# A state-space stage with four input products turned by TensorE and six C products on GpSimd

## The reference

```
u, z   = split(layernorm(x_mod) @ W_in.T)          # 512 + 512 channels
u      = silu(causal_conv4(u))
dt_in, B, C = split(u @ W_x.T, [64, 16, 16])
dt     = clamp(softplus(dt_in @ W_dt.T + b_dt))     # 512
h[n]   = exp(-A[n] * dt) * h[n] (token before) + (dt * u) * B[n]
y      = sum over n of h[n] * C[n]  +  D * u
out    = (y * silu(z)) @ W_out.T, then residual and gate
```

## Time and profile before

| | us |
|---|---|
| median of three runs | 4106.91 |
| profiled execution, first to last instruction (the page gives no other time for it) | 4108.2 |
| DVE busy in the span | 3549.2 |
| POOL busy | 2624.4 |
| PE busy | 3305.6 |
| ACT busy | 2321.0 |

### The profile page before, as it was taken

How to read it: one execution, slowest core, us unless ns; L and a number is a source line. 1 busy time by engine, 2 the same in 40 slices (tenths; PEclk the granted TensorE clock), 3 DMA queues, 4 the chain that set the end, 5 groups by cost and what they waited for, 6 DMA issues and landing times. The chain is left out here.

```text
span 4108.2 us, 61159 instructions
## 1 busy us (share of the span) xinstructions
PE 3305.6 (80%) x21708; PEld 1529.2 (37%) x21708; DVE 3549.2 (86%) x5829; ACT 2321.0 (56%) x4302; POOL 2624.4 (64%) x2459
## 2 busy tenths in 40 slices
PE   5979999999993999999566777777777777776467
PEld 3633333333332555555322232222232232222166
DVE  5768888888854999999359999999999999999967
ACT  5626666666672344444356666666666666666422
POOL 1102323232232888888369999999999999998723
PEclk8969999999996999999888888888888888887689
DMA  4894565655513111110112222212222222222132
GB/s 146 281 188 64 78 84 79 88 80 81 82 33 89 35 44 45 44 48 30 34 44 61 63 65 64 69 47 60 69 65 64 65 69 61 68 57 53 42 95 85
DMA packets 274957, 299.58 MB, mean 73 GB/s; under 512 B 35583, under 2 KB 205686, under 8 KB 274646
## 3 DMA queue, kind: packets, MB, share of 16 engines
q1 hardware_dynamic: 274654, 295.68, 31.4%
HBM read 210.22 MB, written 84.51 MB: 72 GB/s over the span
## 5 line engine op out<-in xcount | busy, mean ns | idle before, releaser
L1727 POOL TENSOR_TENSOR d_dBu<-d_dtu,d_Bn 128x1024 f32<-128x1024 f32 x512 | 1217.5, 2413 | 0.1
L1562 ACT ACTIVATE d_dA<-d_dt,d_decay 128x512 f32<-128x512 f32 x1024 | 690.9, 687 | 404.4 <-DVE d_h L1810 402.1
L752 ACT ACTIVATE b_P<-b_pT 128x512 f32<-128x512 f32 (+1 forms) x1120 | 571.8, 575 | 298.1 <-PE b_pT L658 295.3
L1810 DVE TENSOR_TENSOR_SCAN d_h<-d_dA,d_last_h,d_dBu 128x512 f32<-128x512 f32 x512 | 617.1, 1265 | 14.5 <-ACT d_dA L1562 12.8
L1810 DVE TENSOR_TENSOR_SCAN d_h<-d_dA,d_dBu 128x512 f32<-128x512 f32 x512 | 586.3, 1204 | 40.3 <-ACT d_dA L1562 39.0
L785 DVE CUSTOM_DVE_ANT_0 b_pS<-b_pS,mask_qk 128x512 f32<-128x512 f32 (+1 forms) x768 | 501.7, 690 | 83.6 <-PE b_pS L668 74.3
L630 POOL TENSOR_SCALAR_AFFINE_SELECT b_P<-b_P 128x128 f32<-128x128 f32 (+2 forms) x608 | 192.8, 321 | 515.0 <-ACT b_P L752 503.2
L668 PE MATMUL b_pS<-KS,QS 99*128 99x512 bf16 (+3 forms) x1536 | 475.0, 339 | 28.5 <-PEq L85 21.6
L658 PE MATMUL b_pT<-QS,KS 118*128 118x512 bf16 (+3 forms) x1536 | 449.1, 329 | 3.1 <-ACT b_P L752 2.1
L1817 DVE TENSOR_TENSOR d_h<-d_h,d_C 128x2048 f32<-128x2048 f32 x192 | 434.4, 2262 | 0.7 <-PE d_C L1446 0.7
L1446 PE MATMUL d_C<-d_bc,d_pick 96*128 96x512 bf16 x256 | 114.6, 448 | 396.1 <-DVE d_h L1817 396.1
(11 more groups left out here) (313 smaller groups left out, 5983.2 us busy)
## 6 DMA issues: line engine op xcount, KB each, us to landing
d_Bn<-scratch_bs SPq DMA_DIRECT2D x128, 512.0 KB, 4.9
scratch_parts<-a_part SPq DMA_DIRECT2D x48, 512.0 KB, 4.1
QS<-scratch_parts SPq DMA_DIRECT2D x192, 128.0 KB, 7.4
KS<-scratch_parts SPq DMA_DIRECT2D x192, 128.0 KB, 7.9
scratch_v<-a_v SPq DMA_DIRECT2D x16, 1024.0 KB, 7.7
V<-scratch_v SPq DMA_DIRECT2D x32, 512.0 KB, 11.7
a_x<-in_L_attn_x_dram SPq DMA_DIRECT2D x16, 512.0 KB, 7.7
scratch_o<-b_O SPq DMA_DIRECT2D x16, 512.0 KB, 10.0
```

Of the source, the lines that this page charges most:

```text
L752: act.activation(t[:, heads[0]:heads[-1] + 1, c * CH:c * CH + w], pT[:, place % RING, 0:len(heads) * w].rearrange("p (h w) -> p h w", w=w) ...
L1562: act.activation(dA[:, m % 2, :], dt[:, c.k % 2, m, :], ACT.Exp, scale=decay[:, m, n:n + 1]).then_inc(dA_d, 1)
L1727: pool.tensor_tensor(product(c, n)[:, 2 * j:2 * j + 2, :], dtu[:, c.k % 2, 2 * j:2 * j + 2, :], Bn[:, n // BG % 2, n % BG, :].unsqueeze(1) ...
L1810: dve.tensor_tensor_scan(h[:, n % HS, m, :], dA[:, m % 2, :], product(c, n)[:, m, :], start, ALU.mult, ALU.add).then_inc(scanned, 1)
```

## The change

Four states, PE_B = (5, 8, 11, 14), get their product dtu * B[n] another way. dtu is turned once per chunk into [token, channel] layout: PE makes 16 transposes of 128x128 into the y banks (`turn_step`), ACT copies them to `dtuT` in two parts (`put_step`), and B likewise goes through pC into `BT` (`turn_b`, `put_b`). In that layout B[n] is one number per partition, so the product of a state is four instructions of [128, 512] with a scale per partition: by ACT for states 8 and 14 (`stage_product`), by POOL's `tensor_scalar` for 5 and 11. PE then turns each product back, 4 transposes for each m, into the slots of `dA` in PSUM (`turn_product`), and the decays of the two first m of such a state go to a new SBUF tile `dAs` (as do the others of that state). The scan reads decays from `dAs` and products from `dA`.

POOL_C becomes (0, 3, 6, 8, 10, 12). The C rows for POOL no longer come from pC by ACT but by DMA from scratch (`bs` now holds C too) into three slots `Cn`. `modulate` goes from DVE to POOL, joined with `shift`. x2e is gone: `finish` adds into h1, and SP loads x2 into h1 only after the front's second norm. The orders of all engines are rewritten: ACT has one turn function per m, with entries behind each; PE has three places in a turn; POOL's `weigh` is behind the entries of its turn. The masks of attention go to another allocation scope, which moves addresses.

```diff
-POOL_C = (0, 3, 6, 11)
+PE_B = (5, 8, 11, 14)
+POOL_B = tuple(n for n in range(NS) if n not in PE_B)
+POOL_C = (0, 3, 6, 8, 10, 12)
+LAG, KEEP, AHEAD = 2, 1, (7, 5, 4, 1)
+POOL_P = (5, 11)
+ACT_P = tuple(n for n in PE_B if n not in POOL_P)
@@ SP
+            def spread_c(at, j):
+                slot = at.times(NPC, j) % CR
+                row = NS + POOL_C[j]
+                wait(sp, hC_pool, at.times(NPC, j + 1 - CR))
+                sp.dma_start(Cn[:, slot, :], S["bs"][row:row + 1, tokens(at)].to_broadcast([P, CH])).then_inc(cn_in[slot], 16)
...
                     for g in range(2):
                         if c is not None:
-                            wait(sp, dBu_d, c.times(2 * NS, 2 * (NS - BG + BG * g)))
+                            wait(sp, dBu_d, c.times(2 * NPB, MADE[NS - BG + BG * g]))
                         spread_b(q, g)
+                        if g == 0:
+                            spread_c(q, CR - 1)
                 if e is not None:
+                    wait(sp, xn2, min(total, e.times(1, 4)))
+                    wait(sp, h1_st, 16 * min(total, e.times(1, 4)))
+                    sp.dma_start(h1[:, :, :], tiles(S["x2"][tokens(e), :])).then_inc(x2_in, 16)
                     wait(sp, x3_d, e.times(1, 1))
-                    sp.dma_start(tiles(S["x3"][tokens(e), :]), x2e[:, :, :]).then_inc(stored, 16)
+                    sp.dma_start(tiles(S["x3"][tokens(e), :]), h1[:, :, :]).then_inc(stored, 16)
@@ PE
+            def turn_step(c):
+                wait(pe, dtu_d, c.times(1, 1))
+                wait_before(pe, yz_d, c.times(1, 0), passed)
+                for t in range(CT):
+                    for m in range(MD):
+                        last = pe.transpose(y[:, t, m * P:(m + 1) * P], dtu[:, c.k % 2, m, t * P:(t + 1) * P], K["ident"][:, :])
+                    if t % 2:
+                        last.then_inc(dtuT_mm, 1)
+            def turn_product(c, n, halves):
+                i = PE_B.index(n)
+                if n in POOL_P:
+                    wait(pe, staged_pool, c.times(CT * len(POOL_P), CT * POOL_P.index(n) + CT))
+                else:
+                    wait(pe, staged, c.times(CT * len(ACT_P), CT * ACT_P.index(n) + CT))
+                for m in halves:
+                    wait(pe, scanned, c.times(NS * MD, MD * n + m - 1))
+                    for t in range(CT):
+                        last = pe.transpose(dA[:, m % 2, t * P:(t + 1) * P], product(c, n)[:, t, m * P:(m + 1) * P], K["ident"][:, :])
+                    last.then_inc(turned_b, 1)
@@ PE order
             run(pe, spread,
+                ({},
+                 {1: turn_b, 2: own_input},
+                 {1: lambda q: project(q, IN + 3, 3), 4: lambda q: convolve(q, 1), 9: lambda q: project_dt(q, 2), 13: lambda q: (project(q, GT + 1, MD + 1), project(q, GT + 2, MD + 2))},
+                 {15: lambda f: turn(f, 1)}),
+                sums_dve,
                 ({6: lambda e: output(e, 0)},
+                 {},
+                 {1: lambda q: convolve(q, 0), 4: lambda q: convolve(q, 2), 5: lambda q: convolve(q, 3), 7: project_x, 14: lambda q: project(q, GT + 3, MD + 3)},
+                 {14: lambda f: turn(f, 0)}),
+                sums_pool,
                 ({10: lambda e: output(e, 1)},
+                 {1: turn_step},
+                 {0: lambda q: project(q, IN + 2, 2), 8: lambda q: (project_dt(q, 0), project_dt(q, 1)), 9: lambda q: project_dt(q, 3), 11: lambda q: project(q, GT + 0, MD + 0)},
+                 {15: lambda f: (project(f, IN, 0), project(f, IN + 1, 1))}))
@@ ACT
+                for of in ACT_P:
+                    if MD * n + m in [MD * of - back for back in AHEAD]:
...
+                        act.activation(product(c, of)[:, t, :], dtuT[:, t, :], ACT.Identity, scale=BT[:, t, of:of + 1]).then_inc(staged, 1)
...
-                 {3: lambda f: normalise(f, 0, (0, 1)), 10: lambda f: normalise(f, 1, (0,)), 11: lambda f: normalise(f, 1, (2,)),
+            run(act, decays(0),
+                ({},
+                 {2: put_b},
+                 {1: lambda q: inner(q, 2), 4: lambda q: convolved(q, 1), 8: take_x, 9: lambda q: below(q, 0), 13: lambda q: gate(q, 1)},
+                 {9: lambda f: normalise(f, 1, (0,)), 14: lambda f: normalise(f, 1, (3,)), 15: lambda f: turned(f, 0)}),
+                decays(1),
                 ({0: last_gate},
+                 {},
+                 {3: lambda q: convolved(q, 0), 6: lambda q: convolved(q, 3), 7: silu, 8: split_hi, 9: lambda q: below(q, 1), 10: lambda q: (below(q, 3), grow(q)), 11: split_mid, 14: lambda q: gate(q, 2)},
+                 {5: lambda f: normalise(f, 0, (0, 1)), 13: lambda f: normalise(f, 1, (2,)), 15: lambda f: turned(f, 1)}),
...
+                 {2: lambda c: (put_step(c, 0), put_step(c, 1))},
@@ POOL
+                if n in POOL_P:
+                    wait(pool, scanned, before(c, n))
+                    wait(pool, dtuT_put, c.times(2, 2))
+                    wait(pool, bt_put, c.times(1, 1))
+                    for t in range(CT):
+                        pool.tensor_scalar(product(c, n)[:, t, :], dtuT[:, t, :], BT[:, t, n:n + 1], None, ALU.mult).then_inc(staged_pool, 1)
+                for j in range(2 if n in POOL_B else 0):
...
+            def modulate(f):
+                wait(pool, m_in[f.k // 2 % 2], f.over(4, 16, 16))
+                wait(pool, xn1, f.times(1, 1))
+                pool.tensor_tensor(x[:, :, :], x[:, :, :], row(f, CA), ALU.mult).then_inc(h_mul, 1)
...
             def finish(e):
-                wait(pool, e_in, e.times(32, 32))
+                wait(pool, x2_in, e.times(16, 16))
                 wait(pool, ag_d, e.times(2, 2))
-                pool.tensor_tensor(x2e[:, :, :], x2e[:, :, :], h1e[:, :, :], ALU.add).then_inc(x3_d, 1)
+                pool.tensor_tensor(h1[:, :, :], h1[:, :, :], h1e[:, :, :], ALU.add).then_inc(x3_d, 1)
@@ DVE
                 for m in range(MD):
-                    if m % 2 == 0:
-                        wait(dve, dBu_d, c.times(2 * NS, 2 * n + m // 2 + 1))
+                    if n in PE_B:
+                        wait(dve, turned_b, c.times(MD * NPE, MD * PE_B.index(n) + m + 1))
+                    elif m % 2 == 0:
+                        wait(dve, dBu_d, c.times(2 * NPB, MADE[n] + m // 2 + 1))
```

More of the change, by code:

```diff
@@ L1356, in step @@
                         else:
-                            for chunk, parts in zip((e, q, f), turn):
+                            for chunk, parts in zip((e, c, q, f), turn):
                                 if chunk is not None and n in parts:
@@ L1403, in step @@
[L1403 to L1412, removed]
+                for n in range(NS):
+                    if n == 0 and f is not None:
+                        load(f)
+                    if c is not None:
+                        if n % BG == 0 and 0 < n < NS - BG:
+                            spread_next(c, n // BG + 1)
+                        for j in range(CR, NPC):
+                            if POOL_C[j - CR] + 3 == n:
+                                spread_c(c, j)
+                    if n == 8 and f is not None:
+                        wait(sp, h1_d, f.times(1, 1))
+                        sp.dma_start(tiles(S["r"][tokens(f), :]), h1[:, :, :]).then_inc(h1_st, 16)
+                    if n == 10 and q is not None:
+                        wait(sp, act_read, q.times(NF, WX + 1))
+                        sp.dma_start(S["bs"][:, tokens(q)], xb[DR:DR + 2 * NS, :]).then_inc(b_st, 16)
@@ L1836, in stats @@
                 last.then_inc(stat, 1)
-            def modulate(f):
-                wait(dve, m_in[f.k // 2 % 2], f.over(4, 16, 16))
-                wait(dve, xn1, f.times(1, 1))
-                dve.tensor_tensor(x[:, :, :], x[:, :, :], row(f, CA), ALU.mult).then_inc(h_mul, 1)
             def clear(f):
@@ L1872, in gate_out @@
                 dve.tensor_tensor(h1e[:, 2 * j:2 * j + 2, :], pf[:, :].rearrange("p (t d) -> p t d", d=D), row(e, GA, 2), ALU.mult).then_inc(ag_d, 1)
-            run(dve, scan, weigh_before,
-                ({1: gate_y, 6: lambda e: gate_out(e, 0), 11: lambda e: gate_out(e, 1)},
+            run(dve, scan,
+                ({},
+                 {},
                  {9: split_rest, 12: split_lo},
-                 {4: modulate, 6: stats, 13: clear}))
+                 {6: stats, 10: clear}),
+                weigh_before,
+                ({1: gate_y, 6: lambda e: gate_out(e, 0), 10: lambda e: gate_out(e, 1)},
+                 {},
+                 {},
+                 {}))
     release(nc, sems)
```

194 lines of the change are left out of this document (113 added, 81 removed).

## The result

| | before | after |
|---|---|---|
| median, us | 4104.97 (4102.59 to 4107.72, 4 runs) | 4145.23 (4141.34 to 4189.48, 4 runs) |
| profiled span | 4108.2 | 4140.1 |
| ratio to before | | 1.0118, 95% interval 1.0072 to 1.0165 |

The change makes the kernel about 1% slower. I had forecast 4017 and given "slower" 0.05; the time lies 83 us above the end of the range. The ratio takes in all four runs after, the one at 4189.48 too; the other three lie at 4141.34 to 4148.64, 0.9% to 1.1% above the median before.

What follows compares the result with a forecast made beforehand. DVE was taken as the bound, POOL close behind. From the 4108.2 us span: 69.8 less for weighs, 28.9 less for modulate, plus 2.4 and 6, gives 4018; 4017 as median, range 3986 to 4062.

Steps and rivals of the forecast that it cites:

- the price of tensor_scalar: POOL's eight [128, 512] instructions per chunk for turned products, taken at 0.75 us each, 6.0 together.
- POOL's round: POOL's time per chunk: 103.0 us of work plus 2.0 waiting for x2, 105.0; bounds 103.0 to 110.6.
- the gaps of DVE: DVE's stalls on ACT and PE per chunk: 3.0 us, as before the change; bounds 1.2 and 6.
- DVE's work: DVE per chunk without gaps: 109.6 us less 4.4 for two weighs and 1.7 for modulate, 103.5.
- Scans with a product in PSUM: DVE scans of turned states, decay in SBUF and product in PSUM: extra cost taken as 0.
- Rival 1: POOL becomes the bound, tensor_scalar at 1.2 making its round 108.6 us: 4045 us, chance 0.16.
- silu: ACT's 6.3 us entry behind the second decay of turn 7, making DVE stall 1.1 us per chunk.
- turn 5: First turned state: PE's transposes come behind a sum and a convolution, DVE stalls 0.9 us.
- the turned scans: Other DVE scans awaiting PE's transposes: hidden at full clock, 0.1 us lost each at half; 0.5 per chunk taken.
- Turn 10: grow and a copy on ACT behind the second decay, partly covered by split_rest: DVE stalls 0.5 us.
- Rival 2: The clock falls around the turned states, four transposes taking 1.09 us instead of 0.63: 4055 us, chance 0.12.
- +0.4: Allowance per chunk for DVE and POOL catching each other's stalls, raising the period from 106.5 to 106.9 us.

Runs made afterwards that it cites:

- e12: Kernel after with POOL's tensor_scalar cut to 8 elements, split_lo replaced by a fill and x2 loaded early: 4055.79 us, ratio 0.9881.
- e5: Probe ahead of the kernel before: one DVE subtraction [32, 512] beside busy POOL; 0.68 us with a PSUM operand, 2.73 with both in SBUF, 1.46 beside tensor_scalar.
- e1: Kernel after with split_lo's subtraction on DVE replaced by a fill with zeros, same waits: 4095.38 us, ratio 0.9975.
- e4: Kernel after with x2 loaded behind the second batch of B rows instead of the last: 4121.46 us, ratio 1.0037.
- e9: Kernel after, its orders kept, with one tensor_tensor per turned product of POOL, x2 loaded early and both splits on POOL: 4072.74 us, ratio 0.9920.
- e3: Kernel after with all four turned products made by ACT, none by POOL: 4089.44 us, ratio 0.9961.
- e8: As e7, but with all turned products on ACT: 4078.00 us, ratio 0.9924.
- e10: As e9, but with all four turned products on ACT: 4083.05 us, ratio 0.9941.
- e7: e6 with split_rest and split_lo moved from DVE to POOL, ACT copying the last into bc: 4071.02 us, ratio 0.9909.
- e6: Kernel after with e2 and e4 together and new places for some entries of ACT: 4096.82 us, ratio 0.9971.
- e2: Kernel after with one broadcast tensor_tensor on POOL instead of four tensor_scalar per turned product: 4091.57 us, ratio 0.9956.
- e11: Second probe, ahead of the kernel before: DVE scans and subtractions shaped like split_lo beside pauseless POOL; none over 4.88 us, 0.68 with a PSUM operand.

## Why the prediction was wrong

Three steps failed: the price of tensor_scalar in POOL's round, the two splits taken to stay as they were (put at nothing), and the gaps of DVE.

- **DVE's work: right.** Forecast 103.5, measured 103.6 (e12). Scans with a product in PSUM: right, no cost.
- **POOL's round: failed.** "I take 0.75, near the one-input row" was bounded above by half a product, 1.2. The instruction takes 1.6 in the kernel and 1.55 by itself (e5). A bound taken from another form (two inputs of the same size) did not bound this one. With the x2 wait at 2.7 on average instead of 2.0 the round is not 105.0 but 112.4, the same as the old period of 112.64. Rival 1 had the mechanism, with a price of 1.2 instead of 1.6. e12 against e1 says what POOL's round cost: 4095.4 - 4055.8 = 40 us, with nearly all of the tensor_scalar work and the wait for x2 taken away together. The range left this out too: it ended at 4062, but POOL's own bound of 110.6, which is 3.7 above 106.9, gives 15 x 3.7 = 56 more than the forecast, 4073.
- **Long instructions with two SBUF operands: a term put at nothing.** split_rest and split_lo were taken to stay as they were. With POOL hardly pausing they take 0.7 to 3.2 in ordinary chunks (split_rest 1.9 on average, before 1.2), and in three chunks split_lo takes 14.5 to 17.2. e1 shows that split_lo is worth 50 us; without the three episodes the kernel after would stand at 4145 - 35 = 4110, at no change. They decided the sign. That such an instruction of DVE waits for the tensor_tensor of POOL under way is shown by both probes. Why it was passed over by five or six in a row is open: the second probe had the same shapes, order and density and did not do it. The traces narrow it. In the kernel after and in e4, five of the six long ones started beside the second half product of a pair, with POOL's weigh following without a pause; no split_lo that started so was short, while the eight beside a second half product behind which POOL paused took 0.7 to 2.7. The sixth (17.18) started beside a first half product, where four others took 0.95 to 1.52. No subtraction of the probes started ahead of such a weigh, and the probes also lacked the traffic of DMA, ACT and PE; no run tells these apart.
- **Gaps of DVE: failed, 3.0 forecast, 6.5 measured with POOL free** (e12), over the 6 that the prediction itself named as wrong. silu, turn 5 and the turned scans were sized about right. Turn 10 was 1.3 to 2.0 instead of 0.5. Turn 4 (1.1 to 1.3 in most chunks of e12, up to 2.7 in e9) and the late y before gate_y (0.65 to 2.1) were missing. I had laid out the turns for ACT's own entries and not followed what an entry waits for: a copy that waits for PE, behind a half-rate sum and a convolution, holds the decay behind it.
- **Rival 2 (the clock falls): wrong.** The granted clock of the stage was 0.90, before 0.86. Of the 236 rows of four transposes that turned a product between 2222 and 3900, 219 took 0.5 to 0.7 and 17 took 0.9 to 1.1. No run here shows the rule of the Trainium skill ("TensorE: Matmul & The Clock Gate", "Part 4: PE-mode transpose") at work; it is not contradicted either, since long matmuls stand close around all of them.

By the Trainium skill ("SBUF — State Buffer", "SBUF: two separate sides") a DVE instruction with two SBUF inputs and a GpSimd one that reads SBUF exclude each other for the whole instruction, whichever starts first. The trace agrees for the 0.68 with an operand in PSUM and for the 2.73 and 4.88 of the probes. It does not agree for the 1.46 of e5, which ended inside a tensor_scalar of GpSimd that reads SBUF; and the 14.50 to 17.18 of the kernel span five or six GpSimd instructions, which the rule as stated does not explain.

From the forecast to the result by way of e12 and e1 (the steps are differences of measured times, so they add up by themselves; what each stands for is the reading): 4017; + 39 to e12, which is the gaps (3.1 more than the 3.4 that the forecast had with its +0.4, 15 times, 47) less 12 for DVE's work (102.7 instead of 103.5, since e12 leaves split_lo out) and a rest of 4; + 40 for POOL's round, the wait for x2 included (e12 to e1); + 50 for split_lo, 35 of it in the three episodes (e1 to the kernel after, 4145). The rest of 4 has no name.

The mends do not add up. With POOL relieved (e3, e8, e10) or split_lo off DVE (e7, e9) the period stays at 109 to 112, because ACT and PE then set gaps of 7 to 10 us, and moving an entry only moves the gap (e6 against e2, e9 against e7). Which order of ACT and PE would bring these below 4 us stays open.

## What to carry to other kernels

Price an instruction that has no row by a run or with bounds from both sides that really are bounds: a form with fewer inputs can be slower than one with more (tensor_scalar 1.55, tensor_tensor 1.01 for the same product on POOL). When work moves to POOL until it hardly pauses, look for DVE instructions with both operands in SBUF: they can now wait for POOL, and an unusually long one in the trace before is a warning and not noise. Where two engines are both above 90%, relieving the first gives what the second and the order of the others let through, here 37 us of 90 in the best complete version.

## What the runs showed of the hardware that was not expected

- POOL tensor_scalar, float32: 1.47 us ([128, 512], immediate), 1.55 (factor per partition), 2.74 ([128, 1024], immediate); tensor_tensor of [128, 1024] 2.32, of [128, 512] with a broadcast factor 1.01. In the kernel a turned product of [128, 2048] took 6.2 to 6.6 as four tensor_scalar and 3.6 to 3.7 as one tensor_tensor.
- A DVE subtraction of [32, 512]: 0.68 with an operand in PSUM; with both in SBUF 2.57 to 4.88 beside tensor_tensor of a pauseless POOL, 1.46 beside its tensor_scalar, and 14.5 to 17.2 in six chunks of two kernels (after and e4).
- POOL paid too: two half products next to such a subtraction took 5.09 together in e11 and 5.13 to 5.15 in the kernel after, against 4.63 to 4.70 alone. Beside the long split_lo they took 4.63 to 4.70: there POOL paid nothing.
